# Grouped-query attention in a two-layer fp32 block: scores as two fp32r parts in row tiles of TensorE, row maxima half a unit ahead, exponentials of 1024 and 512 columns in turn

## The reference, cut to what matters

```python
q = einsum('bsd,ed->bse', x, Wq)   # 32 heads x 8
k = einsum('bsd,ed->bse', x, Wk)   # 8 heads x 8
v = einsum('bsd,ed->bse', x, Wv)   # 8 heads x 8
q, k = _apply_rope(q, k, s)
scores = einsum('bkgqd,bkld->bkgql', qg, k) * SCALE
attn = softmax(scores, axis=-1)
out = einsum('bkgql,bkld->bkgqd', attn, v)
return einsum('bsd,ed->bse', out, Wo)
```

## Time and profile before

| | |
|---|---|
| median of 3 runs | 4268.53 us (4267.6 to 4272.98) |
| the profiled execution | 4277.08 us; its span 4275.2 us; mean granted TensorE clock 0.944 |
| busy share of the span | PE 86%, PEld 65%, DVE 62%, ACT 55%, POOL 18% |
| grouped attention, first to last instruction of its score stage (`ga5m`) | 1854 to 2863.6 us of the span |

### The profile page before, as it was taken

How to read it: one execution, slowest core, us unless ns; L and a number is a source line. 1 busy time by engine, 2 the same in 40 slices (tenths; PEclk the granted TensorE clock), 3 DMA queues, 4 the chain that set the end, 5 groups by cost and what they waited for, 6 DMA issues and landing times. The chain is left out here.

```text
span 4275.2 us, 66025 instructions
## 1 busy us (share of the span) xinstructions
PE 3696.2 (86%) x22804; PEld 2783.1 (65%) x22804; DVE 2636.4 (62%) x5009; ACT 2338.6 (55%) x4937; POOL 762.4 (18%) x864
## 2 busy tenths in 40 slices
PE   7999999992969969658888888886989999999979
PEld 6999999991848858312222222234878888988967
DVE  5666666666336653357666676633378888888853
ACT  5777677773413324126666666652256666766632
POOL 2233433220003410100000000002022323232200
PEclk9999999995989989859999999997989999999989
DMA  1000000000000000020000000002011011101010
GB/s 57 21 21 11 21 21 21 21 1 30 0 17 2 0 3 0 16 54 9 15 15 15 15 8 15 15 3 103 4 51 40 26 40 36 33 33 41 26 60 20
DMA packets 24580, 100.25 MB, mean 23 GB/s; under 512 B 5316, under 2 KB 6084, under 8 KB 18036
## 3 DMA queue, kind: packets, MB, share of 16 engines
q1 hardware_dynamic: 24356, 97.25, 7.0%
HBM read 84.52 MB, written 12.32 MB: 23 GB/s over the span
## 5 line engine op out<-in xcount | busy, mean ns | idle before, releaser
L1420 ACT ACTIVATE ga5m_pr<-ga5m_E 128x512 f32<-128x512 f32 x1024 | 582.2, 596 | 309.5 <-PE ga5m_E L1342 301.1
L1435 DVE TENSOR_REDUCE ga5m_nm<-ga5m_M 128x1 f32<-128x1024 f32 x512 | 597.9, 1218 | 179.4 <-PE ga5m_M L1328 178.9
L352 POOL TENSOR_TENSOR all_X<-all_X,at_part 128x512 f32<-128x512 f32 x256 | 335.2, 1309 | 996.0 <-ACT at_part L532 996.0
L1342 PE MATMUL ga5m_E<-ga5m_Q,ga5m_K 128*128 128x512 bf16 x1024 | 390.3, 393 | 65.8 <-ACT ga5m_pr L1420 51.8
L1328 PE MATMUL ga5m_M<-ga5m_K,ga5m_Q 128*128 128x512 bf16 x1024 | 323.9, 400 | 127.9 <-DMA ga5m_Q<-in_zrows 70.7
L417 PE MATMUL at_A<-all_ident,at_prob 128*128 128x128 f32 x2304 | 340.3, 274 | 30.2 <-ACT at_prob L540 20.9
L1342 PEld LDWEIGHTS ga5m_E<-ga5m_Q,ga5m_K 128*128 128x128 bf16 x1024 | 97.5, 98 | 405.4 <-ACT ga5m_pr L1420 346.9
L417 PEld LDWEIGHTS at_A<-all_ident,at_prob 128*128 128x128 f32 x2304 | 265.1, 140 | 59.0 <-DVE at_q1l L600 25.5
L616 DVE TENSOR_TENSOR at_pT1l<-at_A,at_pT1h 128x512 fp32r<-128x512 f32 (+1 forms) x384 | 235.6, 641 | 64.7 <-ACT at_pT1h L521 58.1
L1355 PE MATMUL ga5m_O<-ga5m_pr,ga5m_Vu 128*32 128x512 f32 x2048 | 270.9, 607 | 0.0
L1328 PEld LDWEIGHTS ga5m_M<-ga5m_K,ga5m_Q 128*128 128x128 bf16 x1024 | 88.5, 99 | 273.6 <-DVE ga5m_nm L1435 133.8
(11 more groups left out here) (328 smaller groups left out, 10660.7 us busy)
## 6 DMA issues: line engine op xcount, KB each, us to landing
at_raw<-in_pack SPq DMA_DIRECT2D x32, 1027.0 KB, 5.6
at_slope<-in_slopes SPq DMA_DIRECT2D x32, 512.0 KB, 4.1
ga5m_Q<-ga_qs SPq DMA_DIRECT2D x48, 192.0 KB
ga_qs<-ga5s_part SPq DMA_DIRECT2D x6, 512.0 KB
ga5m_K<-ga_ks SPq DMA_DIRECT2D x48, 48.0 KB
all_X<-in_x SPq DMA_DIRECT2D x1, 2048.0 KB, 7.2
tq_raw<-in_gu SPq DMA_DIRECT2D x1, 2048.0 KB, 7.6
hw_wug<-in_ug SPq DMA_DIRECT2D x1, 2048.0 KB, 9.7
```

Source lines behind the costliest of these rows:

```text
L352: nc.gpsimd.tensor_tensor(X[:, t:t + 2, :], X[:, t:t + 2, :], part[(i - 1) % 2][:, :, :], ALU.add).then_inc(added, 1)
L1342: nc.tensor.matmul(Eb[e % 2][:, :], K[slot][:, kt * P:(kt + 1) * P], Q[slot][:, j * SEQ + qh * 512:j * SEQ + qh * 512 + 512], start=True, ...
L1420: nc.scalar.activation(pr[e % NR][:, :], Eb[e % 2][:, :], ACT.Exp, scale=scale).then_inc(e_done, 1)
L1435: nc.vector.tensor_reduce(nm[slot][:, k:k + 1], Mb[k % 2][:, :], AX.X, ALU.max, negate=True).then_inc(nm_done, 1)
```

## The change

- **Parts.** Queries and keys are split into two fp32r parts (high, low), with one cast and one subtraction for each block. The operands have 24 rows: high, high, low of the query against high, low, high of the key. In memory they are fp32.
- **Four row tiles.** The 24 rows of head j lie on partitions 32 j to 32 j + 23 of `Q`, and the key's rows are there four times in `K`. With two rows for ones and the two parts of the maximum a key-score matmul has 26 rows of the array, in row tile j. The two matmuls of a row-score item take two tiles, j with `Q` and j + 2 with a second copy `Qx`, in which the heads are moved by two.
- **Halves.** Maxima are made for one half of the queries (16 items) instead of a unit, one in every second step, where a step is one key-score matmul, and the transposed maxima follow ten steps (`LEAD = 10`) before the half's first key score. They and the transposed output go through the two buffers `Mb` in one ring with the row items (`at_step`, `items`).
- **Exponentials.** `Eb` has three banks; ACT takes 1024 columns (two banks) and 512 (one) in turn. `pr` has twelve buffers. `values` follows seven steps behind.
- **DMAs.** All of this stage are issued by POOL: eight for the rows of ones, twelve for each unit (before: seven), eight small ones for each half's maxima (before: three for a unit).
- **No loops.** All 32 halves are written out on each engine. POOL's copy of the values (`Vu`, L1303) is gone; `values` reads `Vx` itself.

The diff, cut to its core:

```diff
-    qs = nc.dram_tensor(f"{name}_qs", (NKV * NQ, 3, HD, TOK), BF16, kind="Internal").ap()
+    qs = nc.dram_tensor(f"{name}_qs", (NKV * NQ, 3, HD, TOK), F32, kind="Internal").ap()
...
+                    for i, (src, m, M) in enumerate(work):
+                        high, low = (part[i][x][0:M, :].bitcast(F32) for x in (0, 1))
+                        out = ks if i == 1 else qs[m * 16:(m + 1) * 16]
+                        sp.wait_ge(cast_done, i + 1)
+                        sp.dma_start(out[:, 0], high).then_inc(stored, 16)
+                        sp.dma_start(out[:, 2] if i == 1 else out[:, 1], high).then_inc(stored, 16)
+                        sp.wait_ge(low_done, i + 1)
+                        sp.dma_start(out[:, 1] if i == 1 else out[:, 2], low).then_inc(stored, 16)
...
+            for h in range(NH):
+                first = PER * (h - 1) - LEAD
+                for r in range(4 * NQ):
+                    at_step.setdefault(first + 2 * r, []).append(("row", h, r))
+                at_step.setdefault(first + PER, []).insert(0, ("max", h, 0))
+                at_step.setdefault(PER * (h + 1) + 9, []).append(("out", h, 0))
...
+            groups = [(e, min(e + (2, 0, 1)[e % 3], NE)) for e in range(NE) if e % 3 != 1]
...
+                    for j in range(NQ):
+                        rows = slice(32 * j, 32 * j + NROW)
+                        pool.dma_start(K[n % 2][rows, :],
+                                     ks[kv, :, :, cols].rearrange("a d n -> (a d) n")).then_inc(q_in[n % 2], 16)
...
+                def maxima(h):
+                    n, _, _, qh = place(h)
+                    pool.wait_ge(split_done, 2 * h + 2)
+                    for x in range(2):
+                        for j in range(NQ):
+                            row = 32 * j + NROW + x
+                            pool.dma_start(Q[n % 2][row:row + 1, qh * 512:(qh + 1) * 512].rearrange("o (a n) -> o a n", n=P),
+                                         mpart[x][4 * j:4 * j + 4, :]).then_inc(max_in, 16)
...
+                        for x, (g, src) in enumerate(((j, Q), ((j + 2) % NQ, Qx))):
+                            rows = slice(32 * g, 32 * g + NROW)
+                            mm = nc.tensor.matmul(out[:, x * 512:(x + 1) * 512], src[n % 2][rows, q0:q0 + P],
+                                                  K[n % 2][rows, x * 512:(x + 1) * 512], start=True, stop=True)
...
+                def key_scores(g):
+                    if g >= 2:
+                        pe.wait_ge(e_done, g - 1)
+                    for e in range(*groups[g]):
+                        h, k = divmod(e, PER)
+                        kt, j = divmod(k, NQ)
+                        n, b, kv, qh = place(h)
+                        if k == 0:
+                            pe.wait_ge(max_in, 16 * 2 * NQ * (h + 1))
+                        rows = slice(32 * j, 32 * j + NROW + 2)
+                        mm = nc.tensor.matmul(Eb[:, e % 3, :], K[n % 2][rows, kt * P:(kt + 1) * P],
+                                              Q[n % 2][rows, qh * 512:(qh + 1) * 512], start=True, stop=True)
+                    mm.then_inc(s_done, 1)
...
+                for t in range(START, END):
+                    if 0 <= t < NE and groups[group_of[t]][0] == t:
+                        key_scores(group_of[t])
+                    for x in at_step.get(t, []):
+                        item(x)
+                    if 0 <= t - 7 < NE and (t - 7) % NQ == 0:
+                        values((t - 7) // NQ)
```

More of the change, by code:

```diff
@@ L1185, in grouped_attention @@
             with Scope(nc, name + "s") as s:
[L1186 to L1190, removed]
+                part = [[s.sb(f"part{i}{x}", [P, TOK], F32R) for x in "hl"] for i in range(3)]
+                cast_done, low_done, stored = s.sem("cast"), s.sem("low"), s.sem("stored")
                 block = s.block()
-                work = [(qf, 0, P), (qf, 1, P), (kf, 0, 64)]
+                work = [(qf, 0, P), (kf, 0, 64), (qf, 1, P)]
@@ L1194, in _ @@
                 @block.scalar
                 def _(act):
[L1196 to L1201, removed]
+                    for i, (src, m, M) in enumerate(work):
+                        nc.scalar.activation(part[i][0][0:M, :], src[0:M, m, :], ACT.Copy).then_inc(cast_done, 1)
@@ L1203, in _ @@
                 @block.vector
                 def _(dve):
[L1205 to L1210, removed]
+                    for i, (src, m, M) in enumerate(work):
+                        dve.wait_ge(cast_done, i + 1)
+                        nc.vector.tensor_tensor(part[i][1][0:M, :], src[0:M, m, :],
+                                                part[i][0][0:M, :].bitcast(F32), ALU.subtract).then_inc(low_done, 1)
@@ L1388, in _ @@
[L1388 to L1399 removed]
+                pe.wait_ge(ones_in, 16 * 2 * NQ)
@@ L1465, in unit @@
-                def unit(b, kv, slot, following):
-                    n = kv + b * NKV
-                    done = 0
-                    for k in range(NST):
-                        for _ in range(M_AT[k] if following else 0):
-                            maximum(n + 1, 1 - slot, done)
-                            done += 1
-                        if k == QT + 2:
-                            output(n, b, kv, 0)
-                        if k == T_AT and following:
-                            split(n + 1, 1 - slot)
-                    output(n, b, kv, 1)
```

333 lines of the change are left out of this document (122 added, 211 removed).

## The result

The changed kernel takes **4396.42 us** (median of four runs, 4367.61 to 4404.11) beside 4269.02 for the kernel before on the same chip: ratio 1.0285 as recorded, 95% interval 1.0236 to 1.0333 (the two medians alone give 1.0298). It is slower by 127 us, where the forecast was 4165 and faster. The profiled execution took 4404.11 us, its span 4402.3, and its mean granted clock is 0.836 (before: 0.944).

The account below looks back on a forecast made before the run. No engine was full; a loop of waits with PE in it bounded the kernel. Halves (768) plus DMA waits (84) made 852 instead of 947.6 us, the opening 8 less: 4165 us, 8-in-10 range 4060 to 4325.

Parts of the forecast that it names:

- PE: TensorE's work in a step: values 1.06 us, score slots of 0.22 us with pairs overlapping 1.0 us, 2.1 us together.
- The step: Time between two calls of the values: 2.6 us, bounded by 2.36 and 3.05; eight steps are 20.8 us.
- What would show it: Signs expected in the profile after, among them steps near 2.6 us, clock 0.95 or more, first exponential near 1907.
- the granted clock falls: Rival, chance 0.09: TensorE stays at 1.2 GHz in the stage, a half takes 38 us, time 4530 us.
- W = 8d - 4.5: Each half's first key score waits W us for eight POOL DMAs costing d each; d 0.90 gives 2.7 us.
- Overlap of row tiles: In the score stage, pairs of score matmuls in different row tiles run at once, 1.0 us of slots a step.
- the bound without it: Upper end for a half if row tiles do not overlap: 27.2 us, time 4230 us, chance 0.12.
- The half of 24 us: One of 32 halves of the score stage takes 24 us instead of 29.6, with 21 and 27.2 as ends.
- ACT: Exponentials of four banks' columns take 2.02 us; a half needs 16.7 us with the output's copy, so it does not bound.
- Opening: Before the halves: first exponential at 1907 rather than 1914.7, 8 us less.
- The turn of the half: Once a half, PE waits for ACT to copy the output, then ACT for PE: 2.3 us with the copy.
- ten steps cover the DMAs: Rival, chance 0.24: POOL issues DMAs like SP, d 0.56, no wait at the halves' first key scores, 4072 us.

Follow-up runs that it names:

- Experiment 9: The changed kernel with row tiles of 64 rows instead of 24 and 26, the other head's rows meeting zeros, whole computation kept: 4108.79 us.
- experiments 1 to 3: Kernel before with scores over 26 rows: 4748.12 us; changed kernel with all scores in row tile 0: 4823.58 us, or over all 128 rows: 4213.58 us.
- experiment 10: The changed kernel with the copy of the output accumulator three key-score positions earlier in ACT's order: 4277.67 us.
- experiment 2: The changed kernel with all scores in row tile 0 (up to 26 rows), so that no two matmuls overlap: 4823.58 us.
- experiment 7: The changed kernel with row tiles of 64 rows, each matmul summing over two heads' rows: 4110.32 us.
- experiment 3: The changed kernel with every score matmul over all 128 rows, so that none overlap: 4213.58 us.
- Experiment 11: The changed kernel with zero-padded 64-row tiles, whole computation kept, and the output accumulator's copy three positions earlier: 4073.96 us.
- experiment 5: The changed kernel with only the key scores over all 128 rows, row scores left in row tiles of 24: 4282.83 us.

## Why the prediction was wrong

**The step that failed** is the clock. *PE* and *The step* took every slot at 0.22 us and the values at 1.06 us, and "What would show it" wanted a clock of 0.95 or more. The trace shows 0.53, slots of 0.42 us and more (2306.53, 2306.95) and values of 1.94. That the clock would stay up rested on the 1.00 within a unit of the kernel before, whose score matmuls use all 128 rows; what fewer rows do to it was not asked. Experiment 9 prices it: nearly the same change at 0.99 has a half of 24.4 us instead of 33.9, and 9.5 x 32 = 304 us lie between.

**The rival "the granted clock falls"** (0.09) is what happened, for a reason it did not have. It argued from pauses and from 17 to 19 us of work in 27. PE was busy 90% of the stage and slow; what counts first is how many rows the matmuls use (experiments 1 to 3), and the place of the copy at the turn adds to it, for a reason that stays open (experiment 10). It said a step of 4.2 to 4.5 us, and 4.1 to 4.5 were seen. Its 4530 was too dear by 134 us: it put the half at 38, and it was 33.9.
By the Trainium skill (TensorE: Matmul & The Clock Gate, Part 1) the clock follows how busy the engine has been. The trace does not bear that out by busy time alone: 0.50 at 588 us busy of 600 in experiment 2, 0.96 at 523 in experiment 7. By the Trainium skill (TensorE: Matmul & The Clock Gate, Part 3) matmuls in different row tiles run at once. The trace agrees: three of them began within 10 ns; its 3.07 times for four tiles was not measured here.

**The DMAs on POOL.** In the term W = 8d - 4.5 it was d that was mis-sized: 0.52 us instead of 0.90, below even the lower bound, SP's 0.56. By the formula W is then nothing, and it is absent, so 84 us were charged for nothing: PE and its weight loads waited for these DMAs 2.5 us in the whole stage. At the high clock it does appear now and then, 6.3 us in six waits in experiment 9.

**Overlap of row tiles**: right, and the bound without it was near (27.2 against 27.8 in experiment 3). At the high clock the overlap is worth 27.8 less 24.4 (experiment 9), 3.4 us in a half. **The half of 24 us**: 24.4 in experiment 9, once the clock is held. **ACT**: an exponential of 1024 columns took 1.02 us, as forecast. **Opening**: the first exponential came at 1901, 6 us before the forecast 1907. The smaller d saves 28 x 0.38 = 10.6 us, but the stage's first DMA began at 1860.8 rather than 1856, after stores that ran from 1831.9 and had been put at 18 us. **The turn of the half** was put at 2.3 us; that PE stands 2.1 us there was in it, but not that the clock depends on the place of the copy.

Had the clock stayed up, the same terms without W give 4072 (the rival in which ten steps cover the DMAs). Experiment 9, the nearest to the change at a held clock, measured 4109: the other terms were good to 1%, and one assumed constant, the clock, cost 7% (4396 against 4109). That experiment 11 came within 2 us of the 4072 is luck: it has an edit that the forecast did not, its halves are shorter (23.4 us rather than 24), and its first exponential, at 1908.0, is ten us later than that rival has it.

## What to carry to other kernels

Before cutting TensorE's matmuls down to a few rows, ask what keeps its clock up: here matmuls of 24 and 26 rows, alone or side by side, left it at 1.2 GHz for nearly all of the stage with the engine 90 to 98% busy, which cost more than the overlap saved. Padding the row tiles to 64 rows with zeros, so that a pair uses the whole array, kept the overlap and the clock, and cost four loads a unit and some clearing at the start. When a matmul of unchanged shape gets longer in the profile after (606 to 1018 ns), look at the granted clock before any wait.

## What was not expected of the hardware

- Clock against rows, 2000 to 2600 us, one matmul at a time: 0.51 (26 rows), 0.62 (64), 0.98 (128) in the kernel before. With overlapping row tiles, in the changed kernel: 0.53 for 24 and 26 rows, 0.96 to 0.99 for 64.
- In row tiles of 26 rows, an earlier copy that takes away a wait of 2.1 us in each half raised the clock from 0.53 to 0.68 and gave 119 us. The same kind of wait (up to 1.6 us) beside 64-row pairs left the clock at 0.99, and taking it away there gave 35 us.
- At 2.4 GHz, matmuls that change between a row tile and all 128 rows start 0.43 us apart (experiment 5), those over 128 rows throughout 0.23 us (experiment 3).
- A full-array bf16 matmul ahead of each row item did not raise the clock (0.52) and cost 0.56 us apiece.
- POOL issues a DMA of 2 KB in 0.52 us (502 to 521 ns), and it lands 1.5 us later, against 0.56 and 1.9 for SP's of 8 KB. A load of 24 rows into `K` costs POOL 0.51 us (96 KB) where it cost SP 0.78 (48 KB).
